# Two first steps reordered: lags between ctx blocks, ctx folded before x, selection's rest in the pair banks

## The reference

```
x = x + autocorrelation(layernorm(x), ctx, ctx)
x = x + ffn(layernorm(x))

autocorrelation, per batch and channel:
  corr = ifft(fft(q) * conj(fft(k))).real       # over the 512 positions
  w, idx = top_k(corr, 12);  w = softmax(w)
  out[pos] = sum over i of w[i] * v[min(idx[i] + pos, 511)]
ffn: scores over 64 experts, the best 16 by softmax, z = x A^T gated, out = z B^T * 2
```

## Time and profile before

| | |
|---|---|
| median of three runs | 2185.45 us (2183.13 to 2188.22) |
| the profiled execution's own time | 2186.2 us |
| its span in the trace | 2184.4 us |
| TensorE, VectorE, ScalarE, GpSimd busy | 97%, 78%, 58%, 72% of the span |
| mean granted TensorE clock | 0.992 of full speed |
| attention part / gated layer | to about 1440 us / from there on |

### The profile page before, as it was taken

How to read it: one execution, slowest core, us unless ns; L and a number is a source line. 1 busy time by engine, 2 the same in 40 slices (tenths; PEclk the granted TensorE clock), 3 DMA queues, 4 the chain that set the end, 5 groups by cost and what they waited for, 6 DMA issues and landing times.

```text
span 2184.4 us, 29122 instructions
## 1 busy us (share of the span) xinstructions
PE 2120.8 (97%) x8896; PEld 1330.5 (61%) x8896; DVE 1697.4 (78%) x4080; ACT 1275.1 (58%) x2805; POOL 1564.6 (72%) x1023
## 2 busy tenths in 40 slices
PE   5899999999999999999999997999999999999999
PEld 2455455455455454554554554788888888888887
DVE  7999999999999999999999998744544444454443
ACT  4577776776776776776756645544444334444431
POOL 6899999999999999999999987543333333333420
PEclk9999999999999999999999998999999999999999
DMA  7132232332333332322321244554444544444431
GB/s 285 65 130 101 102 126 101 105 123 101 115 112 102 121 106 102 122 106 101 111 78 63 103 158 168 193 173 161 162 168 167 173 163 164 162 163 172 163 117 58
DMA packets 110417, 287.49 MB, mean 132 GB/s; under 512 B 7137, under 2 KB 7265, under 8 KB 109281
## 3 DMA queue, kind: packets, MB, share of 16 engines
q1 hardware_dynamic: 110304, 286.19, 37.5%
HBM read 219.06 MB, written 67.11 MB: 131 GB/s over the span
## 4 chain that ended last, share of the span: by engine, by line
PE 76%; POOL 9%; DVE 9%; issue 3%; ACT 2%; DMA 1%; SPq 0%; DVEq 0%; POOLq 0%; ACTq 0%
PE pair L706 11%; PE pair L700 6%; PE out L542 5%; PE out L544 5%; PE out L543 5%; PE z L542 5%; PE z L544 5%; PE z L543 5%; PE evac L592 4%; PE pair L605 4%; PE evac L616 3%; PE evac L617 3%; PE lag L656 3%; PE pair L696 3%; POOL r_f L1611 2%
## 5 line engine op out<-in xcount | busy, mean ns | idle before, releaser
L1667 POOL TENSOR_TENSOR rows<-rows,cin 128x1024 f32<-128x1024 f32 x48 | 116.8, 2434 | 342.8 <-DMA rows<-out_dram 278.0
L706 PE MATMUL pair<-r_f,back 128*128 128x512 f32 x768 | 344.7, 597 | 7.3 <-DVE prod L959 3.9
L1611 POOL TENSOR_TENSOR r_f<-prod 128x1024 f32<-128x1024 f32 x128 | 303.0, 2378 | 14.0 <-DVE prod L957 11.7
L706 PEld LDWEIGHTS pair<-r_f,back 128*128 128x128 f32 x768 | 142.4, 190 | 202.1 <-issue 144.5
L700 PE MATMUL pair<-w_sb,wts 128*128 128x512 f32 x512 | 227.4, 597 | 1.8 <-ACT w_sb L1452 1.8
L1333 ACT ACTIVATE xn<-tp 128x512 f32<-128x512 f32 x97 | 56.9, 586 | 257.5 <-PE tp L561 257.4
L542 PE MATMUL out<-b_hi,zt_hi 128*128 128x512 f32 x508 | 201.6, 397 | 4.1 <-issue 2.3
L544 PE MATMUL out<-b_hi,zt_lo 128*128 128x512 f32 x508 | 198.9, 392 | 0.0
L543 PE MATMUL out<-b_lo,zt_hi 128*128 128x512 f32 x508 | 198.2, 390 | 0.0
L542 PE MATMUL z<-a_hi,xt 128*128 128x512 f32 x496 | 195.8, 395 | 0.0
L544 PE MATMUL z<-a_hi,xt 128*128 128x512 f32 x496 | 193.3, 390 | 0.0
(11 more groups left out here) (209 smaller groups left out, 5503.7 us busy)
## 6 DMA issues: line engine op xcount, KB each, us to landing
out_dram<-att_sb SPq DMA_DIRECT2D x32, 1024.0 KB, 4.2
rows<-out_dram SPq DMA_DIRECT2D x64, 512.0 KB, 3.9
cin<-out_dram SPq DMA_DIRECT2D x64, 512.0 KB, 4.0
xin<-in_x_dram SPq DMA_DIRECT2D x64, 512.0 KB, 4.0
out_dram<-rows SPq DMA_DIRECT2D x64, 512.0 KB, 2.6
vf<-in_ctx_dram SPq DMA_DIRECT2D x31, 1024.0 KB, 5.1
xf<-in_x_dram SPq DMA_DIRECT2D x30, 1024.0 KB, 5.3
stat_in<-in_x_dram SPq DMA_DIRECT2D x27, 1024.0 KB, 5.1
```

The costliest lines, as they stand in the source:

```text
L706: return nc.tensor.matmul(pair_ps[:, bank, :], back[:, 3 * bank + n, :], r_f[:, row, :], start=n == 0, stop=n == 2)
L1611: nc.gpsimd.tensor_tensor(dst, prod[:, slot, 0:2, :], prod[:, slot, 2:4, :], ALU.add).then_inc(add_done, 1)
L1667: nc.gpsimd.tensor_tensor(half, first, second, op).then_inc(c_added, 1)
```

## The change

- TensorE, step 0: negacyclic blocks 0 and 1, lags of tiles 0 and 1, blocks 2 and 3, lags of tiles 2 and 3. Step 1: cyclic part first, then x spectrum, then the blocks.
- `left_in`: in step 0 the rest of tiles 0 and 1 is left in pair banks 0 and 2. So the first two cyclic matmuls of step 1 wait for evacuations (`evac_act` 6, `evac_dve` 2), and each half of the x spectrum waits for a pick (`picked`).
- VectorE, step 0: `evac_sin(1)` comes after stage 0 of tiles 0 and 1; the first statistics of the third quarter still stand behind their stage 5; group 1's `evac_sin(0)` comes before stages 1 to 3 of tiles 2 and 3, instead of after their choice. Step 1: the statistics of r_f come after the sums of tiles 0 and 1.
- ScalarE, step 0: `lag_copies((0, 1))` before the copy of block 2; the copies of group 1's first two cyclic parts before `lag_copies((2, 3))`.
- GpSimd, step 0: group 1's ctx is folded to the end before its x.

```diff
-        def left_in(t):
+        def left_in(i, t):
+            if is_step(i, 0) and t < 2:
+                return pair_ps[:, 2 * t, :]
             return evac_ps[t][:] if t < 2 else lag_ps[t - 2][:]
...
                         if n < 2:
-                            if not is_step(i, 0):
+                            if is_step(i, 1) and n == 0:
+                                pe.wait_ge(evac_act, 6)
+                            elif is_step(i, 1):
+                                pe.wait_ge(evac_dve, 2)
+                            elif not is_step(i, 0):
                                 pe.wait_ge(picked, CT * (i - 1) + n + 1)
...
                     if is_step(i, 1):
                         pe.wait_ge(prod_ready, prod_x(0, n) + 1)
+                        pe.wait_ge(picked, n + 1)
...
-                if is_step(i, 1):
+                if is_step(i, 0):
+                    ctx_cyclic()
                     x_spectrum(0)
                     x_spectrum(1)
+                    ctx_negacyclic((0, 1))
+                    first_corr()
+                    ctx_negacyclic((2, 3))
+                    second_corr()
+                elif is_step(i, 1):
                     ctx_cyclic()
+                    x_spectrum(0)
+                    x_spectrum(1)
                     ctx_negacyclic((0, 1, 2, 3))
...
-                        if t == 0:
+                        if t == 0 and not is_step(i, 0):
                             dve.wait_ge(evac_act, 6 * i + 6)
...
                     if is_step(i, 0):
-                        evac_sin(0, 1, before)
                         statistics(stat_in, 2, 2, (1,))
...
-                    evac_sin(1)
+                    else:
+                        evac_sin(1)
...
                     statistics(stat_in, 2, 2, (2, 3))
-                    dve.wait_ge(stat_loaded, 64)
-                    statistics(r_f, 3, 3)
...
                             sums_of((0, 1))
+                            dve.wait_ge(stat_loaded, 64)
+                            statistics(r_f, 3, 3)
...
+                    elif is_step(i, 0):
+                        topk_stages((0, 1), (0,))
+                        evac_sin(1)
+                        topk_stages((0, 1), range(1, 6))
+                        dve.wait_ge(stat_loaded, 48)
+                        statistics(stat_in, 2, 2, (0,))
+                        for t in (0, 1):
+                            choose(t)
+                        sums_of((2, 3))
+                        topk_stages((2, 3), (0,))
+                        evac_sin(0, 1, before)
+                        topk_stages((2, 3), range(1, 4))
...
+                    if is_step(i, 0):
+                        lag_copies((0, 1))
                     evac_from(0, evac_neg(i, 2), v_neg[cur][:, 3, :])
...
+                    if is_step(i, 0):
+                        for part in range(2):
+                            evac_from(part, evac_cyc(1, part), v_cyc[before][:, part, :])
                     lag_copies((2, 3))
...
                 if is_step(i, 0):
+                    pool.wait_ge(v_half, 2)
+                    nc.gpsimd.tensor_tensor(att_sb[:, 0:2, :], second[:, 0:4:2, :], second[:, 1:4:2, :], ALU.add)
+                    nc.gpsimd.tensor_tensor(att_sb[:, 2:4, :], second[:, 0:4:2, :], second[:, 1:4:2, :], ALU.subtract).then_inc(v_ready, 1)
                     begin_fold_x(1)
                     middle_fold_x(1)
                     end_fold_x(1)
```

More of the change, by code:

```diff
@@ L715, in body @@
                     x_spectrum(0)
[L716 to L721, removed]
+                    ctx_negacyclic((0,))
+                    x_spectrum(1)
                     ctx_negacyclic((1, 2, 3))
@@ L724, in body @@
                     turn_weights()
-                if a and not is_step(i, 1):
+                if a and not (is_step(i, 0) or is_step(i, 1)):
                     first_corr()
@@ L736, in body @@
                     turn_tile(0, 1)
-                if is_step(i, 0) or is_step(i, 1):
+                if is_step(i, 1):
                     second_corr()
@@ L1029, in topk @@
                     else:
-                        if t == 0:
+                        if t == 0 and not is_step(i, 0):
                             dve.wait_ge(evac_act, 6 * i + 6)
                         hold(topk_step[t], topk_at(i, 4))
-                        op = nc.vector.match_replace(left_in(t), top[:, t, 8:16], pick[:, t, :], NEG)
+                        op = nc.vector.match_replace(left_in(i, t), top[:, t, 8:16], pick[:, t, :], NEG)
                     op.then_inc(topk_step[t], 1)
@@ L1041, in pick_weights @@
                     dve.wait_ge(topk_step[t], topk_at(i, 5))
-                    nc.vector.scalar_tensor_tensor(e[:, t, :], left_in(t), NEG, e[:, t, :],
+                    nc.vector.scalar_tensor_tensor(e[:, t, :], left_in(i, t), NEG, e[:, t, :],
                                                    ALU.is_equal, ALU.mult).then_inc(picked, 1)
@@ L1160, in body @@
                         topk_stages((2, 3), (3,))
+                    elif is_step(i, 0):
[10 more added lines that the diff above has]
+                        topk_stages((2, 3), range(1, 4))
                     else:
                         topk_stages((0, 1), range(6))
-                        if is_step(i, 0):
-                            dve.wait_ge(stat_loaded, 48)
-                            statistics(stat_in, 2, 2, (0,))
                         for t in (0, 1):
@@ L1403, in top_exp @@
                                          accum_out=exp_sum[:, t:t + 1]).then_inc(exp_done, 1)
-                if a:
-                    if b and not is_step(i, 1):
+                if a and not is_step(i, 1):
+                    if b:
                         act.wait_ge(prod_ready, prod_w(i - 1, 3) + 1)
@@ L1452, in body @@
                         nc.scalar.activation(w_sb[:, l, :], turned(l), ACT.Copy).then_inc(w_copied, 1)
-                if a:
+                if a and not is_step(i, 0):
                     lag_copies((0, 1))
@@ L1718, in body @@
                     end_fold_x(1)
-                    pool.wait_ge(v_half, 2)
-                    nc.gpsimd.tensor_tensor(att_sb[:, 0:2, :], second[:, 0:4:2, :], second[:, 1:4:2, :], ALU.add)
-                    nc.gpsimd.tensor_tensor(att_sb[:, 2:4, :], second[:, 0:4:2, :], second[:, 1:4:2, :], ALU.subtract).then_inc(v_ready, 1)
                 if is_step(i, GROUPS - 1):
```

## The result

| | before | changed |
|---|---|---|
| median, 7 runs each | 2185.45 us (2183.13 to 2191.19) | 2192.83 us (2191.49 to 2196.64) |
| ratio | | 1.003, 95% interval 1.002 to 1.004 |
| span of the profiled execution | 2184.4 us | 2193.6 us |
| group 1's products start (VectorE) | 64.34 us | 71.04 us |
| step 3 starts (TensorE) | 142.68 us | 149.35 us |

The account below looks back on a forecast made before the run. It took the chain through VectorE, nearly full from 40.78 us, and GpSimd as the bound before step 3. -1.86 + 0.66 + 3.4 + 6.0 - 1.95 = +6.25, later +7.1, gave 2192.5 us; range 2186.5 to 2195.5.

Parts of the forecast that it names:

- wait for it: VectorE, step 0: waits from 48.12 to 51.5 us for the third quarter's statistics load, +3.4 us.
- wait for block 1: VectorE, moved sine evacuation: reached at 57.5 us, waits until TensorE's block 1 is ready at 63.5, +6.0 us.
- products of group 1: VectorE: group 1's products start at 70.6 us, +6.3 us.
- Early lags, and the queue behind them: Step 0: lags' sums 1.86 us earlier, sine evacuation +0.66; SyncE issues the statistics' load at 44.3 instead of 40.24 us.
- Group 1's order: ctx before x: x spectrum waits for picks, 52.8 us; two blocks start at 58.1, +1.8 for a lowered clock.
- The evacuation in the queue: VectorE: evacuation ahead of stages 1 to 3 waits 6.0 us for block 1; old waits of 1.61 and 0.34 go.
- The statistics of r_f: Step 1: moved statistics cost 1.7 us on the third product; 0.6 to 0.8 remains after the fourth's wait for GpSimd.
- Step 2: Selection to 101.43 us: all follows VectorE, so +7.1 us is passed on; clock saving taken as 0.
- bound of -1.8 for the clock: Start of step 2: TensorE's shorter idle time could save the slow stretch; bounds -1.8 and 0, 0 taken.
- (b): Rival: statistics land in time, clock full, x at 51.85 us is the bound; +2.4 us, 2187.9 us, chance 0.16.
- (d): Rival, start of step 2: not slower if VectorE's two new waits total under 5.35 us; 2184.9 us, chance 0.10.
- price of -3.0: Rival (d), step 2: no clock loss (-1.8) and no VectorE wait for GpSimd at the last weight product (1.24).

Follow-up runs that it names:

- e5: Changed kernel with SyncE asking for the third quarter's statistics load ahead of group 2's ctx in step 0; ratio 1.0011 to the kernel before.
- e6: Kernel before with only the early lags (with ScalarE's copies and VectorE's block 3 evacuation moved to suit); ratio 1.0018 to the kernel before.
- e2: Changed kernel with group 1's first sine evacuation put back behind the choice of tiles 2 and 3; ratio 1.0014 to the kernel before.
- e3: Changed kernel with the edits of e1 and e2 together; ratio 0.9994 to the kernel before.
- e4: As e3, with r_f's statistics also put back before the first weight product; ratio 0.9987 to the kernel before.
- e9: Kernel before, unchanged, profiled once more; one run, products at 63.36 us, step 3 at 142.18 us.
- e1: Changed kernel with tile 0's third-quarter statistics and their load wait moved to the end of step 0's selection; ratio 1.0016 to the kernel before.
- e8: Changed kernel with six unused matmuls added in two TensorE gaps before group 1's x spectrum; ratio 1.0034 to the kernel before.
- e11: e4 unchanged, run and profiled once more; ratio 0.9987 to the kernel before, step 3 at 137.79 us.

## Why the prediction held, step by step

The forecast was +7.1 us. The first pair of traces gives +6.67 at step 3, the pairs with the repeats 5.9 to 7.2, the medians 7.4. The mechanism is the one forecast: two new waits of VectorE, one for the statistics' load and one for block 1, and both pass on to everything behind them. The terms, by the first pair:

| term | forecast | measured |
|---|---|---|
| VectorE comes to the third quarter's statistics | 48.12 | 48.13 (52.88 less the wait) |
| issue of their load; landing | 44.3; 51.5 | 44.43; 52.83 |
| wait for it | 3.4 | 4.75 |
| wait for block 1; it is ready | 6.0; 63.5 | 5.17; 64.1 |
| products of group 1 | +6.3 | +6.70 |
| first maximum of group 1 | +7.1 | +7.57 |
| step 3 | +7.1 | +6.67 |

- **Early lags, and the queue behind them.** Right in mechanism and in the issue time; e5 and e6 show it. The landing was mis-sized: I took 7.2 us from the issue and the load took 8.4, just outside the end of 8.2 that I gave. My reason was that the small load between had less left to do. It had not: by the sums of issue and duration the three loads landed at 44.0, 45.8 and 48.4 in the kernel before and at 47.6, 50.2 and 52.8 in the changed one. The statistics came 2.6 us behind the small load in both; the small load itself came 2.7 us behind ctx instead of 1.7. Why is open. The small load in the kernel before, issued at 39.86:

```profile
v_last<-in_ctx_dram SPq DMA_DIRECT2D x1, 256.0 KB, 5.9
```

- **Group 1's order.** The x spectrum had to wait for the picks, as forecast (54.37 instead of 52.8, by the landing). Wrong was where the clock is low. I put +1.8 on the two blocks and none on the x spectrum; the x spectrum ran mostly at half clock (+2.7) and the blocks at full. As ScalarE's copy, ready by 59.4 to 59.5, would have held the blocks anyway, about 1.1 of the 2.7 reached the path (60.51 less 59.4). That block 1 is only 0.6 later than forecast is luck: the load was 1.3 us later, and the clock cost 0.7 less, in another place. In the repeat the blocks started at 59.72, with next to nothing of it on the path.
- **The evacuation in the queue.** Right: e2 takes it back and 4.7 us at the products go with it, e3 takes back both and 9.8 go.
- **The statistics of r_f.** I had 1.7 on the third product and let GpSimd absorb all but 0.6 to 0.8 at the fourth, as GpSimd would be done by about 93.9. The edit wasn't tried on the changed kernel itself, but its rows bear the forecast out: from the products to the first maximum it is 26.24 us instead of 25.37, and GpSimd's second weight sum ends at 94.45, so at most about 0.6 us of the fourth product's start at 95.01 is due to the move (an estimate from these two rows):

```profile
92.11 2.34 POOL L1636 TENSOR_TENSOR r_f<-prod 128x1024 f32<-128x1024 f32 x1
95.01 1.21 DVE L966 TENSOR_TENSOR prod<-pair,v_cyc 128x1024 f32<-128x1024 f32 x1
```

  In e3 and e4 the move costs 1.70, because there GpSimd begins group 1's sums 3.4 us behind the products instead of 4.7 (64.62 in e4, 75.70 in the changed kernel) and so absorbs less. The price of the move is one of the kernel around it.
- **Step 2.** I left the bound of -1.8 for the clock unused; the first pair of traces has the four records in 1.98 instead of 3.62. That is why step 3 is at +6.67 and not at +7.6. But the kernel before runs them in 1.98 too (e9), and at step 3 they are worth 0.9, not 1.8. So the change didn't save this stretch, and +6.67 is low by chance: against the repeat of the kernel before the first trace has +7.23 at the first maximum and +7.17 at step 3.
- **Rivals.** (b) is the trace of e1 and e5, where the statistics don't hold VectorE: +2.6 and +1.7 where I had +2.4. (d) needed the two waits together under 5.35 us; they were 9.9. Its price of -3.0 is wrong as well: VectorE's wait for GpSimd at the last weight product is still there (1.25 at 139.97, 1.24 before), and the slow stretch is worth 0.9 at most.

On the two places of the Trainium skill: "DMA: Bandwidth & Descriptors", section "Two DMAs through the same engine are not ordered", says that descriptors start in order and that, when a later one completes, an earlier one has been read but perhaps not yet written. I took that too far: it is no reason for a load to land as if nothing were ahead of it. Here the three loads landed in the order of issue, 47.6, 50.2 and 52.8. That the clock has two levels ("TensorE: Matmul & The Clock Gate", Part 1) agrees with the 0.50 in both stretches at 52.5 to 58.2 us and the 1.00 at 106 to 111.

## What to carry to other kernels

When a step is moved on one engine, look for the first instruction of each other queue that waits for it: here TensorE's later block delayed a load that the change never mentions, because SyncE issues in order, and 1.8 us won at 39 us became 4.75 us of waiting at 48. An evacuation moved ahead in a full engine's queue must come after the time at which its producer is done, not only after its place in the order; the same evacuation waited 0.34 us where it stood. Work set between two dependent steps of a busy engine (r_f's statistics) costs what nothing else that is late there absorbs: 1.70 us in one kernel, about 0.6 in the other. And before a difference of under 1 us between two traces is explained, profile the same kernel twice: the slow stretch that seemed saved here was missing in the repeat of the kernel before as well.

## What was not expected of the hardware

In the changed kernel TensorE's granted clock was 0.50, its lower level, from 52.5 to 58.2 us, around a burst at 54.37 us ahead of which it had done only two matmuls (four records) since 45.8 us and was idle for 2.60 us. It was 1.00 when six unused matmuls filled the gaps (e8).

The length of a gap doesn't tell the clock behind it. After 2.74 us of idle time the four records at 48.68 are listed with 3.09 us in the changed kernel, with 3.62 in its repeat and 3.64 in e1, all longer than at full clock. With the same TensorE work up to there and the same gap, e3 has them at full clock, as have e4, e5 and e11:

```profile
48.82 1.98 PE L598 MATMUL evac<-att_sb,fwd 128*128 128x512 f32 x4 [2.75 <-ACT v_cyc L1378]
```

At the start of step 2 gaps of 1.53 us (changed kernel), 1.57 (e9) and 2.28 (e6) left the four records at 1.98 us, one of 2.50 in the first profile of the kernel before didn't (3.62). What decides between the two is not shown.
